# Later message products, gathers by the source indices in place, two count banks, 192-column node products, and gathered rows for 42 groups of the second layer

## The reference

```python
def _mlp(h, W, b, gamma, beta):
    h = jax.nn.relu(h @ W + b)
    mu = jnp.mean(h, axis=0)
    var = jnp.mean(jnp.square(h - mu), axis=0)
    return gamma * (h - mu) * jax.lax.rsqrt(var + EPS) + beta
# layer 0, on h = relu(layernorm(x))
node_feat = _mlp(x, W_node, b_node, g_node, beta_node)
edge_feat = _mlp(edge_attr, W_edge, b_edge, g_edge, beta_edge)
message = jnp.concatenate([x[row], x[col], edge_feat], axis=1)
message = _mlp(message, W_msg, b_msg, g_msg, beta_msg)
agg = jax.ops.segment_sum(message, col, num_segments=node_feat.shape[0])
return agg + node_feat
# layer 1, on h = relu(layernorm(x)), with dinv = rsqrt(degree)
features = segment_sum((h @ W_gcn)[src] * dinv[src] * dinv[dst], dst)
update = jax.nn.relu(features @ W1 + b1) @ W2 + b2
return x + update
```

## Time and profile before

| | |
|---|---|
| median of 3 runs | 7662.83 us (7657.39 to 7690.72) |
| the profiled execution's own time | 7676.02 us |
| its span | 7674.2 us |
| mean granted PE clock over the span | 0.702 of full speed |

### The profile page before, as it was taken

The page is one execution under the profiler, slowest core; times in us unless marked ns, Lnnn a source line. Parts: engine busy times, 40 slices in busy tenths (PEclk is TensorE's granted clock), DMA queues, the critical chain, the costliest instruction groups (busy, mean ns, idle before and its releaser), DMA issues. The chain is left out here.

```text
span 7674.2 us, 127785 instructions
## 1 busy us (share of the span) xinstructions
PE 5336.5 (70%) x34546; PEld 3643.4 (47%) x34546; DVE 4190.5 (55%) x13388; ACT 4709.8 (61%) x11022; POOL 3260.8 (42%) x3411
## 2 busy tenths in 40 slices
PE   7544436666666666666666666666657999999998
PEld 5211114444444444444434444444445677777777
DVE  4555564444444344444444444444445699999997
ACT  3454535555555555555555555555554499999997
POOL 3555545555555555555555555555555200000000
PEclk7555556666666666666676666666675599999998
DMA  4333322223222222232223222322232111111111
GB/s 158 105 97 93 96 72 71 70 69 87 69 69 71 85 70 69 70 88 71 71 70 88 70 71 71 86 72 69 70 87 69 37 68 68 68 68 68 68 68 69
DMA packets 315566, 586.38 MB, mean 76 GB/s; under 512 B 129522, under 2 KB 185858, under 8 KB 306546
## 3 DMA queue, kind: packets, MB, share of 16 engines
q1 hardware_dynamic: 202882, 324.53, 13.3%
q0 software_dynamic: 103344, 158.83, 9.8%
q10 hardware_dynamic: 8640, 94.84, 3.1%
HBM read 426.94 MB, written 150.87 MB: 75 GB/s over the span
## 5 line engine op out<-in xcount | busy, mean ns | idle before, releaser
L977 POOL DMA_INDIRECT gbuf<-a_tab,idxb x2688 | 2601.7, 968 | 2157.9 <-ACT idxb L968 1048.7
L1077 DVE TENSOR_TENSOR pre<-psum,gbuf 128x384 f32<-128x384 f32 x806 | 449.3, 557 | 2203.0 <-remote 1388.9
L1183 PE MATMUL psum<-x_all 128*128 128x294 bf16 x1260 | 477.8, 379 | 1367.1 <-ACT x_all L1194 860.9
L1064 PE MATMUL psum<-rhs,lhs 128*128 128x96 f32 x6448 | 1317.1, 372 | 27.0 <-ACT lhs L1038 19.8
L1064 PEld LDWEIGHTS psum<-rhs,lhs 128*128 128x128 f32 x6448 | 1202.7, 278 | 130.2 <-issue 55.7
L1108 PE MATMUL psum<-msg,oh 128*128 128x388 f32 x1612 | 1062.1, 755 | 216.2 <-ACT msg L1085 171.0
L1085 ACT ACTIVATE msg<-pre 128x384 f32<-128x384 f32 x806 | 419.9, 521 | 1282.4 <-DVE pre L1077 741.8
L1892 PE MATMUL psum<-x_all 128*128 128x294 bf16 x5208 | 1059.5, 289 | 51.6 <-DVE x_all L1885 16.2
L1183 PEld LDWEIGHTS psum<-x_all 128*128 128x128 bf16 x1260 | 142.2, 113 | 1925.1 <-issue 1032.5
L1884 DVE TENSOR_SCALAR x_all<-x_all,dstrel 128x588 bf16<-128x588 f16 x2604 | 959.4, 368 | 88.6
L1118 ACT ACTIVATE x_all<-psum 32x97 f32<-32x97 f32 x3224 | 776.7, 241 | 335.2 <-remote 245.8
(11 more groups left out here) (230 smaller groups left out, 7499.6 us busy)
## 6 DMA issues: line engine op xcount, KB each, us to landing
adj_tab<-x_all ACTq DMA_DIRECT2D x60, 1543.5 KB
gbuf<-a_tab,idxb POOLq DMA_INDIRECT x3224
x_all<-dst_row SPq DMA_DIRECT2D x806, 64.0 KB
x_all<-attr_parts SPq DMA_DIRECT2D x807, 36.0 KB
x_all<-attr_parts SPq DMA_DIRECT2D x403, 72.0 KB
x_all<-adj_tab SPq DMA_DIRECT2D x30, 945.0 KB
nf<-adj_tab SPq DMA_DIRECT2D x30, 882.0 KB
spilled<-gbuf SPq DMA_DIRECT2D x134, 192.0 KB
```

The source lines that it names most:

```text
L977: g.indirect_dma_start(gbuf[:, k % 4, t, :], None, a_tab[:, :], bass.IndirectOffsetOnAxis(ap=idxb[:, k % 4, t:t + 1], axis=0)).then_inc(g_ ...
L1064: ins = pe.matmul(ps_m(k)[:, t, :], lhs[:, k % 2, t * TILE:(t + 1) * TILE], rhs[:, k % 2, :], start=True, stop=True)
L1183: pe.matmul(bank[7][:, 0:HB], low_e[:, n % 2, :], key_e[:, n % 2, b * HB:(b + 1) * HB], start=True, stop=True).then_inc(n_mm, 1)
```

## The change

It has six parts.

1. `node_products`: one product of 192 columns for each tile in place of two of 96; the two DVE copies read from two banks with a stride.
2. Gathers read their indices from `src_i` itself, in the edge stage and in the message stage. `spill_indices`, `copy_indices` and `idxb` are gone.
3. The order in the message stage: the message product comes two steps after the edge product, the sum over edges four, the fold six; relu of the edge features one step after its product. DVE begins a step with the addition.
4. Early counts: both halves of a tile go to banks 6 and 7 in one go, and ACT copies both in one instruction. Every fourth group is early (28 groups), of the first 112.
5. The last 42 groups (218 supertiles) are not counted. The layer stage also writes the 32-column rows to a table `t_tab` in HBM (`layer_row` on ACT, `layer_row_store` on SP, 64 KB a chunk), and in the counting stage POOL gathers rows of it (872 instructions of 128 rows of 128 bytes, ring of `TR` = 4), and PE adds them up with one-hots: one batch for every `TSTEP` = 8 tiles.
6. So 84 groups (1764 tiles) are left in the counting stage, and early sums run in two windows of three, before in two of four.

```diff
+TAIL = 42
+TR = 4
-        self.early = [g for g in range(4, self.NG, 5)][:self.SV // EARLY]
-        self.late = [g for g in range(self.NG) if g not in self.early]
+        self.counted = self.NG - TAIL
+        self.early = [g for g in range(3, self.counted, 4)][:self.SV // EARLY]
+        self.late = [g for g in range(self.counted) if g not in self.early]
+        self.first = self.counted * GT // SUP
+        self.NTB = self.SV - self.first
...
                 rows = every(lhs[0:C, k % 2, :], t)
-                pe.matmul(ps_chunk(4 + k % 2)[:, t, :], rows, wab[:, 0:C], start=True, stop=True)
-                ins = pe.matmul(ps_chunk(6 + k % 2)[:, t, :], rows, wab[:, C:2 * C], start=True, stop=True)
+                ins = pe.matmul(bank[4 + 2 * (k % 2) + t // 2][:, t % 2 * 2 * C:(t % 2 + 1) * 2 * C], rows, wab[:, :],
+                                start=True, stop=True)
...
             if msgs.absent(i, k) or was_spilled(k):
                 return
-            g.wait_ge(idx_ok.sem, idx_ok.at((MT - MT // SPILL) * i + k - k // SPILL))
             g.wait_ge(m_pre.sem, m_pre.at(MT * i + k - 4))
             g.sem_inc(turn, 1)
+            first = (MT * i + k) * SUP
             for t in range(SUP):
                 g.indirect_dma_start(gbuf[:, k % 4, t, :], None, a_tab[:, :],
-                                     bass.IndirectOffsetOnAxis(ap=idxb[:, k % 4, t:t + 1], axis=0)).then_inc(g_land[k % 4], 16)
+                                     bass.IndirectOffsetOnAxis(ap=src_i[:, first + t:first + t + 1], axis=0)).then_inc(g_land[k % 4], 16)
...
             pe.wait_ge(d_ok.sem, d_ok.at(MT * i + k))
-            pe.wait_ge(s_add.sem, s_add.at(MT * i + k - 1))
+            pe.wait_ge(s_add.sem, s_add.at(MT * i + k - 2))
+            pe.wait_ge(m_pre.sem, m_pre.at(last_message(MT * i + k + 2)))
             pe.matmul(ps_f(k), diag[:, k % 2, :], sel, start=True, stop=True).then_inc(f_mm.sem, 1)
...
             dve.wait_ge(f_mm.sem, f_mm.at(MT * i + k))
+            dve.wait_ge(m_mm.sem, m_mm.at(last_message(MT * i + k + 4)))
...
+            pe.wait_ge(n_oh, n + 1)
+            if n:
+                pe.wait_ge(n_ok, n)
+            for b in range(2):
+                ins = pe.matmul(bank[6 + b][:, 0:HB], low_e[:, n % 2, :], key_e[:, n % 2, b * HB:(b + 1) * HB],
+                                start=True, stop=True)
+            ins.then_inc(n_mm, 1)
...
                     def step(i, k):
                         edge_product(pe, i, k)
-                        early_counts(pe, MT * i + k - 1, 1)
-                        message_product(pe, *msgs.earlier(i, k, 1))
-                        sum_edges(pe, *msgs.earlier(i, k, 2))
-                        early_counts(pe, MT * i + k, 0)
-                        fold_blocks(pe, *msgs.earlier(i, k, 4))
-                    msgs.run(pe, step, 4)
+                        fold_blocks(pe, *msgs.earlier(i, k, 6))
+                        message_product(pe, *msgs.earlier(i, k, 2))
+                        early_counts(pe, MT * i + k)
+                        sum_edges(pe, *msgs.earlier(i, k, 4))
+                    msgs.run(pe, step, 6)
...
                     def step(i, k):
-                        copy_indices(act, i, k)
-                        edge_relu(act, *msgs.earlier(i, k, 2))
-                        early_keep(act, MT * i + k - 3, 1)
-                        early_store(act, MT * i + k - 3)
+                        early_keep(act, MT * i + k - 1)
+                        early_store(act, MT * i + k - 1)
+                        edge_relu(act, *msgs.earlier(i, k, 1))
                         message_relu(act, *msgs.earlier(i, k, 3))
-                        early_keep(act, MT * i + k - 2, 0)
                         square(act, *msgs.earlier(i, k, 3))
-                        keep_blocks(act, *msgs.earlier(i, k, 4))
-                    msgs.run(act, step, 4)
+                        keep_blocks(act, *msgs.earlier(i, k, 5))
+                    msgs.run(act, step, 5)
...
                     def step(i, k):
+                        add_gathered(dve, *msgs.earlier(i, k, 2))
                         onehot_T(dve, i, k)
                         window_rows(dve, i, k)
-                        onehot(dve, i, k)
-                        add_window(dve, *msgs.earlier(i, k, 5))
-                        add_gathered(dve, *msgs.earlier(i, k, 1))
                         early_keys(dve, MT * i + k + 1)
                         early_onehots(dve, MT * i + k + 1)
-                        accumulate(dve, *msgs.earlier(i, k, 2))
-                    msgs.run(dve, step, 5)
+                        accumulate(dve, *msgs.earlier(i, k, 3))
+                        add_window(dve, *msgs.earlier(i, k, 6))
+                        onehot(dve, *msgs.earlier(i, k, 1))
+                    msgs.run(dve, step, 6)
...
+        def layer_row(act, i, k):
+
+            if layer.absent(i, k):
+                return
+            c = 2 * i + k
+            act.wait_ge(p_hid.sem, p_hid.at(c))
+            act.wait_ge(p_t.sem, p_t.at(c - 2))
+            if c >= 2:
+                act.wait_ge(o_t[k], 16 * i)
+            act.activation(t_row[:, k, :, :], ps_t(k), ACT.Copy).then_inc(p_row.sem, 1)
...
+        def tail_gather(g, b):
+            if b >= TR:
+                g.wait_ge(t_mm, b - TR + 1)
+            first = (d.first + b) * SUP
+            for t in range(SUP):
+                g.indirect_dma_start(g_rows[:, b % TR, t, :], None, t_tab[:, :],
+                                     bass.IndirectOffsetOnAxis(ap=src_i[:, first + t:first + t + 1], axis=0)).then_inc(t_land[b % TR], 16)
...
+        def tail_product(pe, b):
+            n = b * TSTEP
+            pe.wait_ge(t_oh, b + 1)
+            pe.wait_ge(t_land[b % TR], 16 * SUP * (b // TR + 1))
+            if n >= 3:
+                pe.wait_ge(a_ok, n - 2)
+            for t in range(SUP):
+                ins = pe.matmul(ps_tail(b), g_rows[:, b % TR, t, :], o_tail[:, b % 2, t, :], start=(t == 0), stop=(t == SUP - 1))
+            ins.then_inc(t_mm, 1)
...
                             if w < ND:
-                                tile_counts(pe, w * GT + j)
+                                n = w * GT + j
+                                if n % TSTEP == 0 and n // TSTEP < NTB:
+                                    tail_product(pe, n // TSTEP)
+                                tile_counts(pe, n)
```

More of the change, by code:

```diff
@@ L1721, in step @@
                     layer_store(sp, i, k)
-                layer.run(sp, step, 0)
+                    layer_row_store(sp, *layer.earlier(i, k, 4))
+                layer.run(sp, step, 4)
                 sp.wait_ge(p_t.sem, p_t.at(NCH - 1))
@@ L1813, in step @@
                     layer_own(act, *layer.earlier(i, k, 7))
+                    layer_row(act, *layer.earlier(i, k, 7))
                 layer.run(act, step, 7)
@@ L1870, in gnn_kernel, with tails_added, late_added @@
         BJ = 7
+        NTB = d.NTB
+        TSTEP = ND * GT // NTB
+        g_rows = sq[:, :, :, :].rearrange("p b t c -> p (b t c)")[:, 0:TR * SUP * H].rearrange("p (b t c) -> p b t c", b=TR, t=SUP)
+        o_tail = oh[:, 2:4, :, :]
+        t_land = [sem(f"t_land{k}") for k in range(TR)]
+        t_oh = sem("t_oh")
+        t_mm = sem("t_mm")
+        t_add = sem("t_add")
+        def tails_added(n):
+            return min(NTB, max(0, -(-(n - 3) // TSTEP)))
+        def late_added(n):
+            return min(ND, max(0, (n - 6) // GT - 1))
@@ new lines, in tail_add @@
+        def tail_add(dve, b):
+            n = b * TSTEP + 3
+            base = dve.value_load(base_i[:, d.first + b:d.first + b + 1], min_val=0, max_val=N - 1)
+            dve.wait_ge(t_mm, b + 1)
+            dve.wait_ge(a_ok, b * TSTEP + 1)
+            if b >= 1:
+                dve.wait_ge(t_add, b)
+            if late_added(n):
+                dve.wait_ge(w_add, late_added(n))
+            if early_added(n):
+                dve.wait_ge(hw_add, early_added(n))
+            nodes_of = sT[0:H, bass.ds(base, W)]
+            dve.tensor_tensor(nodes_of, nodes_of, ps_tail(b), ALU.add).then_inc(t_add, 1)
@@ L1988, in _ @@
                     g.memset(adj[1][:, :, QS:P], 0.0).then_inc(a_zero, 1)
+                    for b in range(NTB):
+                        tail_gather(g, b)
                 @block.tensor
```

142 lines of the change are left out of this document (80 added, 62 removed).

## The result

The changed kernel takes 7467.3 us (median of 4 runs, 7461.1 to 7478.4), the kernel before 7676.8 beside it (4 runs); the ratio is 0.973, 95% interval 0.970 to 0.976. That is 209 us faster, where 6960 and some 700 were forecast: the direction held, the gain was forecast more than three times too large. The profiled execution has a span of 7459.3 for 7674.2.

What follows compares the result with a forecast made beforehand. Message stage paced by waits (PE's signals late beside POOL's gathers), counting by ACT's copies. Terms -21 - 25 - 334 + 4 - 327 = -703 gave 6973 profiled, 6960 median; forecast range 6750 to 7200, wider range 6600 to 7500.

Steps and rivals of the forecast that it cites:

- Counting: Counting stage: fewer tiles counted, POOL's gathers the new bound, 1174 us against 1501: -327, bounds -413 and -280.
- The granted clock of 0.91: Counting stage sign of a wrong forecast: granted clock under 1.00, perhaps from fp32 products; at 0.50 PE would need 2100 us.
- Rival B: PE's signals late in the counting stage too, until POOL's ring is full: +210 there, median 7497; chance 0.2.
- Both arguments against it: Against late counting signals: L1194 waits for "remote" only 190.7; edge stage shows ACT paced by PE's products during bursts.
- Messages: Message stage: indices in place and new order shorten POOL's pauses, 5.47 us a step: -334, bounds -115 and -505.
- the form of the prediction: Message stage: a cycle of q supertiles takes 5.08 q + pause and covers 1.2 q steps; q 2.5, pause 3.7.
- Node products: Node stage: one 192-column product taken as 0.72 us against 0.93 for a pair: -21, bounds -46 and 0.
- Edge stage: Edge stage: indices in place save 0.8 us in each of 32 index-copy pauses: -25, bounds 0 and -198.
- Layer: Layer stage: row copies and stores hidden under PE, wait for last store and zero row: +4, bounds 0 and +14.
- Rival E: Counting-stage gathers held by DVE's one-hots, 1.65 us each: -30 there instead of -327, median 7257; chance 0.08.
- Rival C: Slower: late signals in the counting stage and message stage unchanged, +168, median 7831; chance 0.10.
- D: Message stage: new order ends the standstill and POOL is full, -1158, median 6136; chance 0.07.

Runs made afterwards that it cites:

- nogather_c: Changed kernel without the counting stage's gathers, products and additions kept (last 42 groups' sums not computed), on a chip with late signals: 6937.5 us, before 7676.5.
- a_copy: Changed kernel with the index copy put back at the head of ACT's message step, chip without late signals: 5813.6 us, ratio 0.934 to the kernel before.
- b_inplace: Kernel before with gathers by indices in place in edge and message stages, no index copies, chip without late signals: 6227.2 us, ratio 0.998.
- b_node192: Kernel before with only the node products of 192 columns, on a chip with late signals: 7614.8 us, before 7676.5.
- paced_b: Changed kernel, each counting-stage gather also waiting until ACT has copied two more tiles, on a chip with late signals: 7339.5 us, before 7676.5.
- paced: Changed kernel, each counting-stage gather also waiting until ACT has copied two more tiles: 5808.3 us without late signals, ratio 0.931 to the kernel before.
- tail2: Changed kernel with 2 groups gathered instead of 42, 28 early, 2604 tiles counted: 6133.4 us, ratio 0.983 without late signals; 7450.3, 0.957 with them.
- after_again: Changed kernel, unchanged, run again on a chip without late signals: 5804.5 us, ratio 0.932 to the kernel before.

## Why the prediction was wrong, step by step

**Counting, -327, measured +192: the step that failed.** It is the sentence "This form supposes that PE's signals arrive in time". It put the lateness of these signals at nothing, and the lateness made the stage 1694 us for the 1174 forecast. The rest of the step is right where the signals are in time: 1174 forecast, 1196 measured, POOL without a pause, at a pitch of 1.042 + 0.30 = 1.34 for my 1.31. It had little to spare: PE needs 0.66 a tile and not 0.60, which is POOL's pace too. With late signals come 498 us more (1694 for 1196). The granted clock of 0.91, one of the signs named for a wrong forecast, did not come from the fp32 products: nogather_c has them all and 1.00. Rival B had the mechanism and nearly the size (+210 for +192; its 7497 for 7467), by a wrong picture in part, so that the match is luck in part: a whole standstill until the ring is full, where the trace shows tiles passing at 1.4 us. I gave it 0.2. Both arguments against it were weak. L1194 waited only 190.7 for "remote", because in the message stage of before it seldom was the first to need PE. The changed order shows it: there the same copy stands at the head of ACT's step, and it waits for "remote" for 1061.6 us.

```profile
L1193 ACT ACTIVATE x_all<-psum 128x588 bf16<-128x588 f32 x588 | 391.6, 666 | 1248.5 <-remote 1061.6 <-issue 122.8 <-PE psum L1180 58.8
```

And in the edge stage ACT needs PE's signal only once in two microseconds, for 0.58 here. Two more waits of before, of ACT's L1118 (245.8 us) and DVE's L1137 (370.7), also ended by "remote", look for PE's signals and for none of a transfer. The rows that decided were those that I had used two paragraphs before.

**Messages, -334, measured -305.** Right in form, and near in size partly by luck. From the trace, bursts went from 330 to 296, and the mean pause between the end of one and the start of the next from 4.3 us to 3.70, just the 3.7 reckoned; but a burst holds 2.27 supertiles, not 2.5. With 2.27 the form of the prediction gives (11.5 + 3.7)/2.72 = 5.59 a step, 4507 in all, or -236. Most of the other 69 us lies in two terms: the 0.30 of issue is counted twice in the form (beyond it, POOL's waits are 1060 in 296 bursts, 3.6 each), and four gathers took 5.04 for 5.08. L1072 still waits 1314.0 for remote: the cause of the pauses stayed and their tail went. Which half of the edit did it (no index copy, or the order) was not tried on a chip with late signals. On one without, the copy costs 9 us and the whole message part gives 60. Of these, 55 are gathers that got shorter (L977 990 ns, L972 970); a_copy has 970 with the copy and b_inplace 994 without it, so they go with the new order, for a reason that stays open. Every sixth supertile is gathered ahead in the edge stage (`SPILL = 6`), and not every fifth, as is written above; the 1.2 steps for each gathered supertile are right.

**Node products, -21, measured -45.** The term lacked the clock. With half the products, each of twice the columns, PE has gaps, and the granted clock from 100 to 130 us rose from 0.56 to 1.00; b_node192 (0.99, stage 104.8) shows that this edit alone does it. Whether the gaps or the fewer weight loads keep the clock up is not shown.

**Edge stage, -25, measured -56,** of which the node part alone brings 11 (b_node192's 912 for 923); against b_node192 on its own chip nogather_c and paced_b have 37 and 48 less. The term was too small: POOL's waits of 198.5 us for copied indices became 129 for SP's store and "remote" (L753), 2.2 us less a pause where I had put 0.8. Without late signals the stage is 725 for 727: POOL waits there 28.3 us for copied indices in the kernel before, and there is hardly a pause to shorten.

**Layer, +4, measured 0.** The copies and stores are hidden, as said.

**Rival E** is out: gathers beside DVE's one-hots took 0.99 us on average (1.04 on the chip without late signals), not 1.65. The Trainium skill ("SBUF — State Buffer", Who interferes with whom) has it that a `tensor_scalar` on DVE, as these one-hots are, can enter a two-port mode and then shuts POOL out for the whole instruction. The trace doesn't bear out such a price: it shows a twentieth to a tenth more than the 947 ns median of the earlier trace rows, and DVE's L1971 at 373 ns for L1884's 368. **Rival C** failed on its message half (the messages gained). **D**'s picture, POOL full in the messages, holds on the chips without late signals, but not for D's reason, the new order: the kernel before has it there as well.

Of the kernels tried, paced does best over both kinds of chip: 7339.5 where the signals are late (changed 7467.3, before 7676.5; one run, on another chip than the changed kernel's) and 5808.3 where they are not (changed 5804.5). tail2 has 0.957 on one chip where they are late, but 6133.4, 329 us more than the changed kernel, where they are not.

## What to carry to other kernels

Before adding POOL's gathers to a stage, look in the trace for what other engines' waits do beside gathers that are there already; a wait named "remote" that ends only after the last gather is a price that the new stage may pay too, and more so the shorter its round trips are. Count a stage's signals and buffers, not only its busy times: three buffers at 0.58 us a tile are 1.74 us in all, and signals that were late by 1.45 (median) made a tile take 1.41 in the third and fourth microsecond of a burst. And take the trace on more than one chip before believing a bound: the same code took 23% longer where one engine's signals were late.

## What was not expected of the hardware

- The same kernel took 7676, 7782 and 6222 to 6236 us on different chips, with near equal durations of the instructions that stand at its waits (L1077 557 and 558 ns, L1085 521 and 521, L977 968 and 990). The difference goes with the time that PE's signals need beside POOL's gathers: L1077 waits 1388.9 us for "remote" on one, and not at all on the others, where gathers run in 5 bursts and not 330. SP's issues of six loads take 7.02 us beside gathers on the one and 2.7 to 2.8 on the other. Whether the gathers' issue or their transfers delay the signals, and what differs between the chips, stays open. Only one chip was met at two times, a quarter of an hour apart, both times without late signals, so it isn't shown either that the lateness belongs to the chip and not to what else ran there.
- PE was busy for all of the 30 us from 100 to 130 us at a granted clock of 0.56, and for 23 of them at 1.00 when one product of 192 columns stood for two of 96.
- In the counting stage, with PE standing between tiles, the granted clock is 0.91 (the result); without the gathers it is 1.00 (nogather_c), and with gathers and signals in time 0.99 (after_again).
